# Finding every edge's record row before the first scatter, two edge columns per product, in a graph-network kernel

## The reference, cut to what matters

```python
h = relu(layernorm(x))
x = x + L0(h)     # msg = relu(h[src] + edge_attr @ We + be); segment_sum(msg, dst); MLP; batch norm
x = x + L1(...)   # two graph convolutions
x = x + L2(...)   # two relational layers: per edge a row of a table by (type, src), summed by dst
x = x + L3(...)   # ten propagation steps
# 6250 nodes of 96 features, 100000 edges (dst sorted, src random), edge_attr of 32 features, 8 edge types
```

## Time and profile before

| | us |
|---|---|
| median of 3 runs | 7528.98 (7528.26 to 7531.79) |
| the profiled execution, its span | 8764.9 |
| in it: first and last scatter (L727) | 156.0 to 1659.7 |
| gathers of L0 (L742, node_table) | 1667.4 to 3326.7 |
| gathers of L2 (L742, relation_table) | 4036.6 to 6696.8 |

### The profile page before, as it was taken

How to read it: one execution, slowest core, us unless ns; L and a number is a source line. 1 busy time by engine, 2 the same in 40 slices (tenths; PEclk the granted TensorE clock), 3 DMA queues, 4 the chain that set the end, 5 groups by cost and what they waited for, 6 DMA issues and landing times.

```text
span 8764.9 us, 139892 instructions
## 1 busy us (share of the span) xinstructions
PE 5477.0 (62%) x45326; PEld 4376.6 (50%) x45327; DVE 2623.9 (30%) x6033; ACT 1597.9 (18%) x3464; POOL 3312.1 (38%) x3295
## 2 busy tenths in 40 slices
PE   4444444246776666895343435443343999999998
PEld 3322222133333334893232324333233999999998
DVE  4100000157776665214222223222224111111111
ACT  1111111002345662012111112111110000000000
POOL 2354545455555550003666662666663000000000
PEclk7555555567777777997666667666665999999999
DMA  6111111252223333443222224222223666666665
GB/s 242 37 45 40 42 41 41 49 62 68 75 80 81 89 88 77 141 156 123 64 62 69 62 70 118 62 69 61 67 64 76 200 198 198 198 199 199 198 198 165
DMA packets 531584, 914.64 MB, mean 104 GB/s; under 512 B 223563, under 2 KB 365916, under 8 KB 530348
## 3 DMA queue, kind: packets, MB, share of 16 engines
q1 hardware_dynamic: 285816, 621.27, 22.9%
q0 software_dynamic: 104896, 162.89, 9.0%
q10 hardware_dynamic: 140646, 128.06, 4.8%
HBM read 705.38 MB, written 205.67 MB: 104 GB/s over the span
## 4 chain that ended last, share of the span: by engine, by line
PE 49%; another core or an unknown queue 21%; issue 15%; DVE 8%; DVEq 3%; ACT 3%; DMA 1%; ACTq 1%; POOL 0%; SPq 0%; POOLq 0%
PE bank L1390 27%; PE bank L1255 5%; PE bank L1244 3%; PE bank L1335 2%; PE bank L1092 2%; DVE edge_sums L1859 2%; PE bank L1416 1%; PE bank L1367 1%; DVE onehot L1774 1%; DVEq L518 1%; PE bank L1154 1%; PE bank L1157 1%; PE bank L1408 1%; PE bank L1142 1%
## 5 line engine op out<-in xcount | busy, mean ns | idle before, releaser
L742 POOL DMA_INDIRECT rows<-relation_table,staged_rows x1664 | 1679.3, 1009 | 1690.7 <-DMA staged_rows<-table_rows_of_tiles 1200.3
L1390 PE MATMUL bank<-own_term,h_transposed 128*128 128x192 f16 x16464 | 1378.2, 247 | 55.4 <-DMA h_transposed<-edge_counts_T 32.9
L1390 PEld LDWEIGHTS bank<-own_term,h_transposed 128*128 128x128 fp8e4 x16464 | 1364.8, 98 | 56.7 <-issue 55.9
L742 POOL DMA_INDIRECT rows<-node_table,records_in x832 | 876.5, 1053 | 789.3 <-PE bank L1244 524.9
L727 POOL DMA_INDIRECT rec_dst<-staged_records,staged_record_rows x781 | 750.2, 961 | 904.5 <-ACT staged_record_rows L850 521.6
L1390 PE MATMUL bank<-own_term,staged_records 128*128 128x192 f16 x12348 | 1032.4, 246 | 0.0
L1390 PEld LDWEIGHTS bank<-own_term,staged_records 128*128 128x128 fp8e4 x12348 | 1020.0, 98 | 0.0
L1859 DVE TENSOR_TENSOR edge_sums<-edge_sums,bank 128x96 f32 x1664 | 421.3, 253 | 1743.6 <-remote 859.7
L1335 PE MATMUL bank<-rows,onehot 128*128 128x96 f32 x3328 | 565.1, 334 | 319.8 <-issue 139.1
L1014 ACT CAST staged_records<-bank 128x512 fp8e4<-128x512 f32 (+1 forms) x637 | 332.7, 566 | 2147.4 <-remote 1245.9
L1335 PEld LDWEIGHTS bank<-rows,onehot 128*128 128x128 f32 x3328 | 525.3, 245 | 374.1 <-issue 364.0
(11 more groups left out here) (329 smaller groups left out, 6220.3 us busy)
## 6 DMA issues: line engine op xcount, KB each, us to landing
h_transposed<-edge_counts SPq DMA_DIRECT2D x280, 784.0 KB, 4.2
staged_records<-edge_counts SPq DMA_DIRECT2D x210, 784.0 KB, 4.2
h_transposed<-edge_counts_T SPq DMA_DIRECT2D x56, 784.0 KB, 4.3
rec_dst<-records_in SPq DMA_DIRECT2D x80, 520.0 KB, 9.7
records_in<-rec_dst SPq DMA_DIRECT2D x104, 400.0 KB
edge_counts_T<-staged_records ACTq DMA_DIRECT2D x343, 112.0 KB
staged_records<-edge_counts_T ACTq DMA_DIRECT2D x49, 784.0 KB
edge_counts<-staged_records ACTq DMA_DIRECT2D x49, 784.0 KB
```

The source lines that it names most:

```text
L742: pool.indirect_dma_start(out=rows[:, g, j, 0:D], out_offset=None, in_=source, in_offset=at(ap=index(g, j), axis=0)).then_inc(gathered[g], 16)
L1390: last = nc.tensor.matmul(banks[j][:, 0:2 * D], slots[c][:, at:at + P], z[:, c * SB + i, :], start=(c == 0 and i == 0), stop=(c == SG - 1 ...
```

## The change

The places of all 18 chunks are found in one go, before the first scatter; then the 71 edge products follow with nothing between them. At the start DVE's and ACT's work is changed so that one product serves two edge columns: the even column's 49 keys stand in partitions 0 to 48, the odd column's in 64 to 112 (ODD, KEYS = 113), in one weight tile. compare becomes one product of 512 columns and two of 256; the look-up becomes one product of 28 columns per pair and two of 7. same gets four PSUM banks and four SBUF buffers, and the one-hots three (KEY_BUFS). POOL clears the rooms of the keys and of the ends at the start. The nodes' norm on DVE follows after all places.

```diff
-QC = 4 * MC
+QC = 44
+ODD = 64
+KEYS = ODD + NB
+WIDE_END = 4 * SG
+KEY_BUFS, SAME_BUFS = 3, 4
...
+            nc.gpsimd.memset(key_room[1], 0.0)
+            nc.gpsimd.memset(key_room[0], 0.0)
+            nc.gpsimd.memset(ends_here, 0.0)
+            nc.gpsimd.memset(ends_there, 0.0).then_inc(keys_zero, 1)
+            pool.wait_ge(ends_lo_ready, 2 * len(pair_ends))
+            nc.gpsimd.memset(key_room[2], 0.0).then_inc(keys_zero, 1)
...
+            def load_blocks(i):
+                q0, n = i * (QC // 2), CHUNK[i] // 2
+                for e in range(2):
+                    first = e * PAIR_COLS + q0
+                    act.dma_start(key_pair[i % KEY_BUFS][e * ODD:e * ODD + NB, 0:n * P],
+                                  block_dram[first:first + n, :].rearrange("(a c) p -> a (c p)", a=1)
+                                  .broadcast_to([NB, n * P])).then_inc(block_row_in[i % KEY_BUFS], 16)
+            act.wait_ge(keys_zero, 1)
+            act.wait_ge(blocks_out, 64)
+            load_blocks(0)
+            load_blocks(1)
             for g in range(SG):
                 act.wait_ge(ends_ready, g + 1)
-                nc.scalar.activation(ends_hi[:, g, :], cell_counts[:, g, :], ACT.Identity, scale=-1.0).then_inc(ends_hi_ready, 1)
+                nc.scalar.copy(counts_pairs[ODD:KEYS, g, :, :], counts_pairs[0:NB, g, :, :]).then_inc(ends_kept, 1)
+            act.wait_ge(ends_kept, SG)
+            for lo, hi, pe_ in pair_ends:
+                for e in range(2):
+                    on = slice(e * ODD, e * ODD + NB)
+                    nc.scalar.activation(pe_[on, :, e, 0, :], counts_pairs[on, :, lo:hi, e].rearrange("p g q -> p q g"),
+                                         ACT.Identity, scale=-1.0).then_inc(ends_kept, 1)
...
+                    if j == 2 and i >= 1 and i - 1 + KEY_BUFS < QCHUNKS:
+                        act.wait_ge(places_ps, i)
+                        load_blocks(i - 1 + KEY_BUFS)
...
-            def body(s, next_columns, after_columns):
-                keep_same((s + 1) * MC, next_columns)
-                act.wait_ge(places_ps, s + 2)
-                if after_columns:
-                    load_blocks((s + 2) * QC, after_columns)
-                act.wait_ge(rows_made, s + 1)
-                for slot in range(RING_S):
-                    keep_edges(slot, RING_S * s + slot, s * (16 * MC))
-                    put_together(slot, (RING_S * s + slot) * MC)
...
+            load_blocks(2)
+            for i in range(QCHUNKS):
+                keep_same(i)
+            act.wait_ge(rows_made, QCHUNKS)
+            for n in range(MCH):
+                keep_edges(n % RING_S, n, n // RING_S * (16 * MC) if n >= RING_S else None)
+                put_together(n % RING_S, n * MC)
+                if n == 0:
+                    std(1)
...
+                for k in range(w // 2):
+                    q = 2 * j + k
+                    last = nc.tensor.matmul(bank[:, 2 * k * P:2 * (k + 1) * P], key_pair[i % KEY_BUFS][:, q * P:(q + 1) * P],
+                                            key_each[i % KEY_BUFS][:, q, :, :].rearrange("p e n -> p (e n)"), start=False, stop=True,
+                                            skip_group_check=True)
...
+                    nc.tensor.matmul(both, key_pair[i % KEY_BUFS][:, q * P:(q + 1) * P],
+                                     ends[0:KEYS, i * (QC // 2) + q - lo, :, :, :].rearrange("p e h g -> p (e h g)"),
+                                     start=True, stop=False, skip_group_check=True)
+                    for e in range(2):
+                        last = nc.tensor.matmul(place_bank(i, 2 * q + e)[:, 0:SG],
+                                                same[n % SAME_BUFS][:, (2 * k + e) * P:(2 * k + e + 1) * P],
+                                                of_group[:, i * QC + 2 * q + e, :], start=False, stop=True,
                                                 skip_group_check=True)
...
+            for n in range(SAME_BUFS):
+                compare(n)
+            for n in range(len(groups)):
+                look_up(n)
+                if n + SAME_BUFS < len(groups):
+                    compare(n + SAME_BUFS)
+            pe.wait_ge(rows_made, QCHUNKS)
...
+            for n in range(1, MCH):
+                edge_product(n % RING_S, n, (n // RING_S + 1) * 16)
                 edge_product_end(n, n)
...
+            def block_columns(i):
+                n = CHUNK[i] // 2
+                pair, each = key_pair[i % KEY_BUFS], key_each[i % KEY_BUFS]
+                dve.wait_ge(block_row_in[i % KEY_BUFS], 32 * (i // KEY_BUFS + 1))
+                for e in range(2):
+                    on = slice(e * ODD, e * ODD + NB)
+                    last = V.tensor_scalar(each[on, 0:n, e, :], pair[on, 0:n * P].rearrange("p (q n) -> p q n", n=P),
+                                           key_no[on, 0:1], None, ALU.is_equal)
+                then(last)
+                V.tensor_scalar(pair[:, 0:n * P], pair[:, 0:n * P], key_no[0:KEYS, 0:1], None,
                                 ALU.is_equal).then_inc(block_T_ready, 1)
...
+            for i in range(QCHUNKS):
+                record_rows(i)
+                if i + KEY_BUFS < QCHUNKS:
+                    block_columns(i + KEY_BUFS)
```

More of the change, by code:

```diff
@@ L70 @@
 assert KN * KC == ECP and KN % 2 == 1
-QC = 4 * MC
-QN = EC // QC
-QL = ECP - QN * QC
-assert QN == 17 and QL == 3 * MC + 1 and QC * SG <= 512
+QC = 44
+QCHUNKS = -(-ECP // QC)
+CHUNK = tuple(min(QC, ECP - i * QC) for i in range(QCHUNKS))
+PAIR_COLS = ECP // 2
+ODD = 64
+KEYS = ODD + NB
+WIDE_END = 4 * SG
+HERE_PAIRS = 330
+KEY_BUFS, SAME_BUFS = 3, 4
+assert ECP % 2 == 0 and all(c % 2 == 0 for c in CHUNK) and NB <= ODD and HERE_PAIRS % (QC // 2) == 0
+assert QC // 4 * WIDE_END <= 512 and QC % 4 == 0
 assert SG * SB == NB and SG == 7
@@ new lines, in _, with compare @@
+            groups = [(i, j) for i in range(QCHUNKS) for j in range(-(-CHUNK[i] // 4))]
+            def compare(n):
+                i, j = groups[n]
+                w = min(4, CHUNK[i] - 4 * j)
+                if j == 0:
+                    pe.wait_ge(block_T_ready, i + 1)
+                if n >= SAME_BUFS:
+                    pe.wait_ge(same_sb, n - SAME_BUFS + 1)
+                bank = same_bank[n % SAME_BUFS]
+                nc.tensor.matmul(bank[:, 0:w * P], ident16[:, :], after[:, 0:w * P], start=True, stop=False,
+                                 skip_group_check=True)
[3 more added lines that the diff above has]
+                                            key_each[i % KEY_BUFS][:, q, :, :].rearrange("p e n -> p (e n)"), start=False, stop=True,
+                                            skip_group_check=True)
+                last.then_inc(same_ps, 1)
@@ new lines, in record_rows @@
+            def record_rows(i):
+                n, c0 = CHUNK[i], i * QC
+                dve.wait_ge(places_ps, i + 1)
+                for half in range(2):
+                    lo, hi = half * HALF_CHUNK, min(n, (half + 1) * HALF_CHUNK)
+                    at_half = place_banks[i % 2][:, half * BANK:half * BANK + (hi - lo) * 2 * SG]
+                    last = V.tensor_tensor(picked[:, lo:hi, :, :], at_half.rearrange("p (c h g) -> p c h g", h=2, g=SG),
+                                           of_group[:, c0 + lo:c0 + hi, :].unsqueeze(2).broadcast_to([P, hi - lo, 2, SG]), ALU.mult)
+                then(last)
+                then(V.tensor_reduce(place_f[:, 0:n], picked[:, 0:n, :, :].rearrange("p c h g -> p c (h g)"), X, ALU.add))
@@ L1672, in _ @@
             block_of_tiles(1)
-            record_rows(1, QC, QC)
-            block_columns(2, QC)
             dve.wait_ge(x_in, 32)
```

242 lines of the change are left out of this document (95 added, 147 removed).

## The result

| | before | after |
|---|---|---|
| median, us | 7529.93 (7528.26 to 7531.79) | 7603.76 (7598.05 to 7608.42) |
| ratio after / before | | 1.0096, 95% interval 1.0084 to 1.0108 |
| profiled execution, its span | 8764.9 (in front), 7525.4 (a second profile, below) | 7606.7 |
| first scatter | 157.6 | 252.3 |
| last scatter | 1179.1 | 1261.1 |

The change costs 74 us, a little under 1%.

What follows compares the result with a forecast made beforehand. It took POOL's scatters to pace the timed stage: first scatter at 428 us, plus 986 and 10, ends at 1424 against 1155, +269 on 7529, say 7800 us. Its own range was 7690 to 7850; 8 in 10, 7350 to 7850.

Steps and rivals of the forecast that it cites:

- The reading of the 1236 us: Traced execution, 1236 us over the median: nearly all of PE's late signals beside scatters are gone in the timed runs.
- The count: Whole kernel before: 4472 us left for scatters and gathers untraced; at POOL's pace and L0's own they need 4381.
- the stretches that were taken over unchanged: Trace outside scatters and gathers, 2942 us, where none of them runs; taken as the same in the timed runs.
- The 91 us that the count left over: 4472 us available against 4381 explained; could lengthen the kernel before's scatter stage from 1155 us to 1246 at most.
- The rival that had the late signals in the timed runs: Scatter stage: late signals real, POOL cheaper untraced, so the change ends faster, at 7407 or 7292 us; chance 0.28.
- The edge stage: Edge products alone after the places: POOL runs through, 986 us plus 10 for one hiccup, ending at 1424 us.
- the price of the places: Before the first scatter, moved from 156.0 to 428 us: 272 us in which POOL has nothing to do.
- One group: Four columns of places on PE: compare 1.08 us plus look-up 0.55, sum 1.63 (1.40 to 1.75); 196 groups 319 us.
- Clock: PE while finding places: granted clock stays at 0.50, 1.2 GHz, for all 196 groups.
- Start: Before the places: ends ready at some 95 us, one-hots 0.93 us each, POOL's memsets free, PE begins at 97.5.
- presort at full clock: Rival on PE's places: 0.82 us a group, 160 us, stage ends at 1265, +110 us, 7640; chance 0.12.
- the round at which the sign turns: Untraced round of 44 scatters in the kernel before: above 69 us or so, the change would be faster.

Runs made afterwards that it cites:

- presort_old_products: The kernel before with its order alone changed: all 18 chunks of places first, old one-column products of 49 key rows; 7881 us, ratio 1.0477.
- before_keys_65_rows: presort_old_products with key products reading 65 rows instead of 49, the added rows zeros; 7720 us, ratio 1.0262 to the kernel before.

## Why the prediction was half right

**The reading of the 1236 us was right.** The count gave an untraced stage that ends at 1155 us, at most 1246; the second profile has it end at 1180, and the stretches that were taken over unchanged last 2943 us for 2942. The steps under it are less exact, and partly made up for each other: L0 took 1280 us for 1315, L2 with its gap 2281 for 2195. The 91 us that the count left over come out as L2's 86; the 35 that the scatters took beyond 986 are balanced by L0's 35 less. Of the 25 us that the stage is longer, POOL's holds by the one-hots are 19 (1.2 us in each of 16 rounds) and three at the end 7.5. The norm cost 10, for which 13 had been taken. The rival that had the late signals in the timed runs, and the change a gain, fell with it.

**The edge stage was right.** Forecast 986 + 10 us from the first scatter; measured 1009: 985, the wait behind ACT's root 9, the norm's holds 9, and 4 at the end. POOL ran through beside the edge products.

**The step that failed is the price of the places; group, clock and start were all wrong in it.** Forecast: PE begins at 97.5, 196 groups of 1.63 us, 319 us, first scatter at 428. Measured: 118.6, 123 us, 252.3.

- *One group.* The step took 1.08 us for compare and 0.091 for each small product from a group of the kernel before, and changed only their number. Ten changes between 49 and 128 rows are in that group, 1.0 of its 2.17 us. The change drops them, because its products read 113 rows; no step of the working uses that depth. At the same clock the group measures 1.02 us, below the lower bound of 1.40. That is 120 of the 319 us. The experiments with 65 and 113 rows show this term by itself.
- *Clock.* The step kept 0.50 from one chunk in which PE was busy 22.5 of 23 us. The new products had the full clock 5.7 us after their start, and kept it to 244 us. Groups then take the 0.59 us of PE's own products, 0.63 in the mean with three waits for one-hots and the slower start: another 77 us. The Trainium skill's rule, cited in the prediction (TensorE: Matmul & The Clock Gate, Part 1), that sustained activity releases the clock, gave here the right rival. It did not hold for the old products: in presort_old_products they worked for 420 us and stayed at 1.2 GHz, and in before_keys_65_rows for 250. The row was true of the products that it was of, and no evidence about others. The measured 7604 lies in the range of the rival, 7580 to 7690, which was given a chance of 0.12.
- *Start.* It came 21 us late. ACT begins the ends only when it has copied the last counts (97.3), and DVE writes its half behind it. Both write through strided views, 4.2 us for 2310 elements where 782 in a row take 0.84 on ACT and 0.89 on DVE: ready at 111.7, not 95. The first one-hots took 2.7 us each, not 0.93, beside POOL's memset of the third room (111.75 to 115.4). The prediction had put POOL's memsets at nothing, or at 10 us if the keys had to wait for them. These rows were read, not tested.

```profile
101.48 8.38 DVE L1636 SCALAR_TENSOR_TENSOR edge_sums<-h_transposed,edge_sums 49x2310 bf16<-49x2310 f32 x2 [5.11 <-ACT edge_sums L882]
111.73 5.35 DVE L1646 TENSOR_SCALAR h<-h,key_of_partition 49x2816 bf16<-49x2816 bf16 x2
```

The rival "presort at full clock" came within 4 us of the stage's end, 1265 for 1261, by luck, since its errors cancelled: a group of 0.82 us that measures 0.63, against a start 21 us too early and scatters 13 us too short. It gave 7640, mostly since the stage before was set 25 us too short. The sum as it should have been: 1261 - 1179 = +82 us, in the two profiles 7606.7 - 7525.4 = +81, in the medians +74. Two slips in the sums change nothing of this: 95 + 2.8 is 97.8 and not 97.5, and the round at which the sign turns is 55.5 + 272 / 17.75 = 71 us at the traced price of a scatter, not 69.

**What the change buys and pays.** In its own terms it works: places that took PE 24 us a chunk take 6.8. But POOL paces the stage in both kernels, the places were hidden beside its scatters already, and 95 us of POOL's time now pass before the first scatter. It gets 13 back in all: no one-hot holds a scatter any more (19), against ACT's wait of 9 for the norm.

## What to carry to other kernels

Ask of every stage which engine paces it in a run that isn't disturbed, and put nothing ahead of that engine's first instruction: here each microsecond ahead of the first scatter was a microsecond of the total, to within a few. Where a trace is longer than the timed runs, take a second one before reading waits off it. And a product's price holds for its depth and its neighbours: before scaling it by a count, look whether the change alters the depth.

## What the runs showed of the hardware

- A change between TensorE products of 49 and of 128 rows costs 0.10 us; between 65 or 113 and 128 rows nothing was to be seen, since products of 7 columns start some 0.03 us apart with a change and without one. Padding 49 rows of keys with 16 rows of zeros brought the first scatter from 536.5 to 366.2.
- Products of 49 rows (420 us without a pause) and of 65 rows (busy 88% for 250 us) ran at 1.2 GHz throughout, by their own times; the same ones with 113 rows got 2.4 GHz for part of the time (0.74 to 0.93 in the mean from 150 to 300 us), and the products of the kernel after for all of it from 124 us on.
- DVE's products over two operands in SBUF, and its one-hots in one, hold POOL's indirect DMA until about their end: 4.75, 7.22 and 13.56 us for 0.96. Its statistics over 96 elements each held none.
- One profiled execution had TensorE's signals some 30 us late in each round and took 1236 us longer than the timed ones; a second profile of the same kernel had none and took the median's time.
